# Attention values of two head groups in one TensorE run with one copy out, gate features and second keys in one run, and all orders laid anew

## The reference

```python
# 1: cross attention, 16 heads of 16, over 64 picked rows (with repeats) of 154 context rows
q = x_q @ W_q.T;  c_kv = x_kv @ W_kv_down.T
kv = c_kv[picks] @ W_kv_up.T                 # keys and values
out = softmax(q . k * SCALE) @ v;  return out @ W_out.T
# 2: gated linear attention, 8 heads of 64, chunks of 64, dense plus one of 4 experts (top 1)
q1, k1, v = x @ Wq, x @ Wk, x @ Wv
q2, k2 = x @ Wqa @ Wqb, softmax(x @ Wka @ Wkb)
gk1, gk2 = log_sigmoid(x @ Wg1a @ Wg1b + bg1) / 16, log_sigmoid(x @ Wg2a @ Wg2b + bg2) / 16
o = gla(q1, k1, v, gk1) + sum_over_experts(gla(q2 * fac, k2 * fac, v, gk2 * mask))
g = x @ Wga @ Wgb
o = o * rsqrt(mean(o * o) + EPS) * norm_w * silu(g);  return o @ Wo
```

## Time and profile before

| | us |
|---|---|
| median of 3 runs | 1137.16 (1136.33 to 1138.87) |
| the profiled execution, its own time | 1137.37 |
| its span, first to last instruction | 1135.8 |
| busy: TensorE / VectorE / ScalarE / GpSimd | 1077.7 / 978.7 / 933.8 / 686.0 |
| mean granted TensorE clock | 0.988 |

### The profile page before, as it was taken

One profiled execution on the slowest core, in us unless ns is written; L12 is line 12 of the kernel. 1 busy time (PEld: TensorE's weight loads), 2 busy tenths in 40 slices (PEclk: granted clock), 3 DMA queues, 4 the chain that ended last, 5 costly groups with the idle time before them and its releaser, 6 DMA issues.

```text
span 1135.8 us, 30935 instructions
## 1 busy us (share of the span) xinstructions
PE 1077.7 (95%) x11840; PEld 872.7 (77%) x11840; DVE 978.7 (86%) x2793; ACT 933.8 (82%) x2322; POOL 686.0 (60%) x707
## 2 busy tenths in 40 slices
PE   2879999999999999999999999999999999999986
PEld 1557888887888788778888887888787788888764
DVE  5679999998899999999999998999899999998652
ACT  2578888888888888888888898888889888888761
POOL 4266555577655556766655677565557666555553
PEclk9889999999999999999999999999999999999998
DMA  5432222223222222223212222222222222121111
GB/s 155 141 124 58 72 52 57 54 70 76 67 68 52 50 57 73 62 70 86 67 43 50 57 67 71 73 71 48 63 57 61 63 68 68 44 52 48 31 32 24
DMA packets 86857, 73.83 MB, mean 65 GB/s; under 512 B 34553, under 2 KB 71743, under 8 KB 86710
## 3 DMA queue, kind: packets, MB, share of 16 engines
q1 hardware_dynamic: 86278, 70.98, 24.4%
q10 hardware_dynamic: 432, 0.89, 0.2%
HBM read 37.43 MB, written 13.94 MB: 45 GB/s over the span
## 4 chain that ended last, share of the span: by engine, by line
PE 79%; DVE 8%; DMA 3%; POOL 3%; ACT 3%; SPq 2%; issue 1%; DVEq 0%; ACTq 0%
PE F L407 8%; PE F L862 5%; PE F L810 5%; PE TM L732 5%; PE F L401 5%; PE F L873 4%; PE F L782 4%; PE F L837 4%; PE TM L739 3%; PE F L797 3%; PE F L867 3%; PE SA L720 3%; PE F L821 3%; PE TM L749 3%; PE F L755 2%; PE F L854 2%
## 5 line engine op out<-in xcount | busy, mean ns | idle before, releaser
L727 DVE CUSTOM_DVE_ANT_0 SA<-SA,LNC 128x154 f32<-128x154 f32 x512 | 146.5, 346 | 16.2 <-PE SA L720 13.0
L2176 POOL TENSOR_TENSOR QREST<-QT,QPARTS 128x256 f32<-128x256 f32 x27 | 18.1, 672 | 174.6 <-ACT QPARTS L1872 174.6
L713 DVE TENSOR_REDUCE PACKED<-HOT 128x19 int32<-128x1216 bf16 x64 | 92.4, 1443 | 0.2
L2194 POOL TENSOR_TENSOR QM<-QD,ISEXPT 128x1024 f32<-128x1024 f32 x27 | 81.9, 3032 | 11.5 <-DMA QD<-QG 11.1
L732 PE MATMUL TM<-CONST,EXPS 128*128 128x128 f32 x512 | 84.5, 288 | 0.4 <-ACT OT L1781 0.4
L732 PEld LDWEIGHTS TM<-CONST,EXPS 128*128 128x128 f32 x512 | 73.9, 207 | 2.0 <-ACT OT L1781 0.7
L2166 POOL TENSOR_TENSOR LS<-LS,ZABS 128x1024 f32<-128x1024 f32 x27 | 64.0, 2371 | 13.5 <-ACT ZABS L1932 13.0
L727 DVE DVE_READ_ACCUMULATOR2_ANT MAXS<- 128x1 f32 x512 | 70.6, 138 | 0.0
L2174 POOL TENSOR_TENSOR LS<-LS,ZABS 128x512 f32<-128x512 f32 x27 | 34.5, 1279 | 54.9 <-ACT ZABS L1840 54.9
L720 PE MATMUL SA<-KNOW,QS 128*128 128x154 bf16 x512 | 56.0, 232 | 10.9 <-DMA KNOW<-k_dram 9.2
L407 PEld LDWEIGHTS F<-XMT,WQ 128*128 128x128 f32 x512 | 63.4, 196 | 2.7 <-issue 1.3
(11 more groups left out here) (541 smaller groups left out, 3813.2 us busy)
## 6 DMA issues: line engine op xcount, KB each, us to landing
QD<-QG SPq DMA_DIRECT2D x128, 128.0 KB, 2.3
QS<-q_dram SPq DMA_DIRECT2D x64, 192.0 KB, 3.3
q_dram<-QPARTS SPq DMA_DIRECT2D x32, 192.0 KB, 2.4
XA<-x_dram SPq DMA_DIRECT2D x32, 128.0 KB, 2.1
QS<-q_dram SPq DMA_DIRECT2D x32, 128.0 KB, 3.3
XB<-x_dram SPq DMA_DIRECT2D x32, 128.0 KB, 3.2
out_dram<-OUT SPq DMA_DIRECT2D x32, 128.0 KB, 1.7
EG<-EGP SPq DMA_DIRECT2D x128, 4.0 KB, 1.8
```

The costliest lines, as they stand in the source:

```text
L713: return dve.tensor_reduce(PACKED[:, r], HOT[:, r, :], AX.X, ALU.add)
L727: last = dve.tensor_tensor_reduce(s, s, LNC[t % 2][:, :], -1.0, LARGE, ALU.add, ALU.min, out[:, h:h + 1])
L2194: pool.tensor_tensor(QM[:, 1, :, :, :].rearrange("p a b t -> p (a b) t"), QD[:, :, :, :].rearrange("p a b t -> p (a b) t"), ISEXPT[d % 2][ ...
```

## The change

- values becomes values_pair: two groups, 16 matmuls behind each other into OUTS2, two neighbouring stretches of 128 columns; ScalarE copies both in one instruction (OT[:, 0:2], OT[:, 2:4]). s_b_values and s_b_ot count two a tile instead of four, in SP's wait for the next batch's keys too.
- half_pairs for the gate and half_rows for k2 become half_pairs_rows, which runs late in the turn: the gate's features into MIDS, k2 into KIDS, columns 256 to 511 of the same two banks. The first run disappears from before kv_products. ScalarE's copy to SG and its following steps move behind it; VectorE's maximum over k2 waits for that copy.
- The lists of all five engines are put in another order, in the first, steady and last turns, and the waits follow. No instruction but those two copies a tile is added or taken out.

```diff
-        OUTS = MA[:, 3 * P:4 * P]
+        OUTS2 = MA[:, 2 * P:4 * P].rearrange("p (n t) -> p n t", t=P)
-        MID, MIDS, MIDD = D2[:, 0:D], F[:, 0:2, 0:D], F[:, 2:4, 0:D]
-        k2_heads = MIDS.rearrange("p a (h d) -> p a h d", d=DK)
+        MID, MIDS, KIDS, MIDD = D2[:, 0:D], F[:, 0:2, 0:D], F[:, 0:2, D:2 * D], F[:, 2:4, 0:D]
+        k2_heads = KIDS.rearrange("p a (h d) -> p a h d", d=DK)
...
-        def values(t, g, pt):
-            o, v = OUTS, VNOW[t // TPB % 2]
+        def values_pair(t, first):
+            v = VNOW[t // TPB % 2]
+            for n in range(2):
+                g, o, pt = first + n, OUTS2[:, n, :], PT[n]
...
+        def half_pairs_rows(pairs_out, rows_out, w_pairs, x0, x1, w_rows, y1, y0):
+            half_pairs(pairs_out, w_pairs, x0, x1)
+            return half_rows(rows_out, y0, y1, w_rows)
```

More of the change, by code:

```diff
@@ L929, in pe_first_tiles @@
                 transposes(D0, flat(KG1T[:, :, :]), NP).then_inc(s_d_k1t_ps, 1)
+                pe.wait_ge(s_d_at1, d + 1)
+                inner(KG2T, QG2).then_inc(s_d_a2_ps, 1)
+                pe.wait_ge(s_d_tokens, 2 * d + 1)
+                transposes(D0, flat(KG2T[:, :, :]), NP).then_inc(s_d_k2gt_ps, 1)
+            if b >= 0:
+                pe.wait_ge(s_b_probs_act, 2 * b + 1)
+                values_pair(b, 0).then_inc(s_b_values, 1)
+            if c == 0:
+                pe_v_rest()
             if c >= 0:
@@ L932, in pe_first_tiles @@
                 v_product(XMT[c % 2]).then_inc(s_c_v_ps, 1)
-            if d >= 0:
[L934 to L960, removed]
+            if b >= 0:
+                pe.wait_ge(s_b_exps2_2, b + 1)
+                scores(b, 3).then_inc(s_b_scores, 1)
+                pe.wait_ge(s_b_ot, 2 * b + 1)
+                exp_transposes(EXPS[:, 0]).then_inc(s_b_exps_ps, 1)
+            if d >= 0:
+                pe.wait_ge(s_d_tokens, 2 * d + 2)
                 pe.wait_ge(s_d_at2, d + 1)
@@ L983, in pe_first_tiles @@
                 state_outputs().then_inc(s_d_o_ps, 1)
+            if c >= 0:
+                pe.wait_ge(s_c_router, 5 * c + 4)
+                pe.wait_ge(s_c_zmin, 2 * c + 2)
+                router_rows().then_inc(s_c_rows_ps, 1)
             if b >= 0:
                 pe.wait_ge(s_b_probs_act, 2 * b + 2)
[L986 to L1014, removed]
+                values_pair(b, 2).then_inc(s_b_values, 1)
             if a >= 0:
@@ L1024, in pe_first_tiles @@
             if d >= 0:
+                pe.wait_ge(s_d_state1, d + 1)
+                pe.wait_ge(s_d_sq, d + 1)
+                pe.matmul(D2, const("pairs"), RMS[:, :], start=True, stop=True).then_inc(s_d_ms_ps, 1)
+            if b >= 0:
+                pe.wait_ge(s_b_ot, 2 * b + 2)
+                transposes(TA, flat(OT[:, :, :]), GROUPS).then_inc(s_b_ot_ps, 1)
+            if d >= 0:
+                dense_kv_products(V[d % 2]).then_inc(s_d_kvd_ps, 1)
+            if c >= 0:
+                if c == 0:
+                    pe.wait_ge(s_vall, 2)
+                pe.wait_ge(s_c_hidg, 16 * c + 16)
+                pe.wait_ge(s_c_hidk, 16 * c + 16)
+                pe.wait_ge(s_c_cume, c + 1)
+                half_pairs_rows(MIDS, KIDS, WG, HID2, HIDG, WKB, HID1, HIDK).then_inc(s_c_k2_ps, 1)
+            if b >= 0:
+                pe.wait_ge(s_b_out, 2 * b + 2)
+                transposes(TA, ON[:, :], KD).then_inc(s_b_ont_ps, 1)
+            if d >= 0:
                 if d == 0:
@@ L1534, in dve_last_tiles @@
+            if b < TILES:
+                dve.wait_ge(s_a_counts_pool, b + 1)
+                maxima(b, MAXS[:, 0, :]).then_inc(s_b_max, 1)
+            dve.wait_ge(s_e_y_ps, e + 1)
+            dve.wait_ge(s_e_store, 16 * e)
+            dve.tensor_tensor(OUT[:, :], MID, X1B[e % 2][:, :], ALU.add).then_inc(s_e_out, 1)
             if c < TILES:
```

1449 lines of the change are left out of this document (711 added, 738 removed).

## The result

The changed kernel takes 1168.03 us (median; 1162.21 to 1170.23), the kernel before 1137.01 us in the same comparison: 1.026 times the time, 95% interval 1.022 to 1.030. The forecast was 1117 us with a range up to 1141: the change was to save 20 us and costs 31, and the measured time lies outside the range.

The account below looks back on a forecast made before the run. TensorE's own instruction list was taken to bound the kernel. 27 turns falling from 32.99 to 32.25 us save 20.0, the ends 1.0: 1137.4 - 21 = 1116.4, written 1117 us, range 1107 to 1141.

Parts of the forecast that it names:

- Part 1: TensorE's list in each steady turn: 22 changes of array split become 19, saving 0.50 us (0.3 to 0.7).
- Part 2: TensorE's list: waits before the gate products (0.24 us) and around ON's transposes (0.15) go, leaving 31.97 us a turn.
- Part 3: VectorE's chain, next to be late: a loop as long as TensorE's list, 0.3 us added, a turn of 32.25 us.
- the loop over VectorE: VectorE's state adds through QG2, then TensorE's inner product to the end of the state outputs: 31.8 to 32.2 us.
- Rival 1: GpSimd's SG product starts first and locks out VectorE's HOT product: 33.4 us a turn, 1147 us in all; chance 0.25.
- part 5: First and last turns: switches lost save 1 us in all; setup moves cost -4 to +6 us, taken as 0.
- Part 4: Queues of SP and GpSimd: earlier z slabs save up to 0.1 us a turn; SG's product ahead of QREST costs nothing.

Follow-up runs that it names:

- the first run: The changed kernel with GpSimd's SG product waiting until VectorE's first one-hot product has ended: 1140.83 us, ratio 1.004 to the kernel before.
- five edits: On the changed kernel: SG's wait, batch pieces behind queries' slabs, gate slabs and indices early, XM ahead of the one-hot product in first turns: 1119.98 us.

## Why the prediction was wrong

**Part 1, fewer changes of split: right, a little high.** The paired values run at 0.24, 0.22, 0.22 us, and three changes put back cost 0.41 us a turn against 0.50. Start to start, the values take 2.02 us a turn in the first run and 2.29 in the kernel before: 0.27 less, 0.28 forecast.

**Part 2, the two waits: right in kind, high as well.** TensorE's list was forecast at 31.97 us, 0.89 less than 32.86. Where nothing disturbs it, it is 32.13, 0.73 less. The gate features, k2, ON and the two products behind them together lose 0.35 us, against 0.22 and 0.15 forecast. Of the 0.25 between the run on WK and what follows it, 0.15 went: it now takes 1.89 us, the same run on WQ 1.78.

**Part 3, the turn of 32.25 us: this step failed.** The sum of the loop over VectorE was right: 31.8 to 32.2 us forecast, some 31.9 measured in the first run (VectorE's stretch 16.4 against 16.3, TensorE's 15.4 against 15.25). But the sum took HOT's first product as unhindered, and in the changed kernel it takes 2.54 us instead of 1.45 in every turn; the clean turn is 33.18 us, not 32.25. The prediction had seen that HOT and SG would meet, had worked out that 0.2 us decide, and gave the bad case 0.25. The row-by-row answer was against HOT: VectorE's Q and KS ended at 641.96, not ScalarE's RSTD2 (641.42), so HOT came at 642.20, SG at 642.02. The sum of VectorE's own list from Q to XM could have been laid beside ScalarE's from RSTD2 to LS's exponential with rows of before; the prediction named this case ("second if its own list brings it there 0.2 us later") and did not decide it. Rival 1's price, 33.4 a turn, was about right: 33.18 clean. That the mean of 33.52 comes nearer to it is luck, because the mean also holds the batch pieces. Its total of 1147 us missed for the ends (part 5). One row behind this rival was read too simply: XN took 1.35 us beside SG, but it has only one tensor in SBUF as input, so the rule for two inputs that the prediction quotes is not about it, and it ended 0.15 us after SG where XM, a product like it, takes 0.40. QM behind HOT's second product is the closer case.

**Part 4, the queues: failed twice.** "SG's product ahead of QREST costs nothing there" holds for GpSimd (QREST still waits 101.6 / 26 = 3.9 us for ScalarE; 6.5 before). This part asked who waits for GpSimd and not whom GpSimd holds up while it runs, which only rival 1 did: 27.2 us. For SP the prediction credited the new order with up to 0.1 us a turn. It looked at the slabs of z, which did get out earlier, and not at the pair that had become tight: scores(a, 0) moved ahead in TensorE's list, to 20.2 us behind the gate products instead of 22.5, while the batch pieces stayed ahead of the queries' store. 9.8 us.

**Part 5, the ends at 0 (-4 to +6): failed.** +17.6 us at the start, three times the bound. The prediction judged the first turns by one wait of VectorE and by the length of two of them; those two together are unchanged (69.1 us against 69.2), and all of the loss lies before them. Three edits together account for 15.6: index loads, gate slabs, and XM behind the one-hot product.

In all, the forecast was 51 us too low; the runs account for 48 of it (1168.0 to 1120.0) by five edits that touch none of what the change is for. What is left, 3 us, is roughly the net of about 5 us in the first turns, whose cause is open, and of a mean turn of 32.20 us, 1.3 us less in 27 turns than forecast.

## What to carry to other kernels

When an order is laid anew, a moved instruction has to be checked in two directions: who waits for it, and which instructions of other engines will now run beside it; VectorE and GpSimd products on SBUF belong in one timeline. Where a meeting is decided by 0.2 us and repeats in every turn, work it out to the end or treat it as the likeliest case, not as a rival. Lists for the first turns are a program of their own: walk each load in them to its first reader.

## What the runs showed of the hardware

- A VectorE product of bf16 in SBUF (128x2496) takes 1.45 us alone, 2.54 behind a GpSimd product begun 0.18 us earlier, 1.97 behind one of half the length. The other way round GpSimd pays: in the first run QREST took 0.97 us behind HOT's second product (0.45 us of overlap), 0.67 in the kernel before. In all three cases the later one loses the overlap less some 0.15 us. The Trainium skill, SBUF — State Buffer, section Who interferes with whom, says that the later of such a pair fully blocks; the trace agrees here but for these 0.15 us.
- A wait added to one engine made the whole 2.3% faster (1168.0 to 1140.8).
- A change of TensorE's split costs 0.14 us on the mean of three (0.13 for one, 0.28 for two, read start to start); single entries in the chain had shown 0.14 to 0.22.
- A 512 KB load issued 0.4 us ahead of a store of 192 KB moved the first read behind that store from 2.6 to 5.6 us after its issue, in the one turn read.
